# Four-layer transformer on one core: semaphores declared in another order, two bits to a bisection step in the last mixture's routing, and gathered rows added inside the fourth batch

## Chip, core and metric

One core of a Trainium2 chip runs the whole program in one launch. The metric is the device time of that launch in microseconds; the time of a kernel is the median of its runs. Engines are called as in the profile: PE is TensorE (PEld its weight loads), DVE is VectorE, ACT is ScalarE, POOL is GpSimd, SP is SyncE, which only issues transfers here.

## What is computed

Four layers in sequence on 4096 tokens of 128 features (4 batches of 1024). Each layer is `x = x + attention(xn) + ffn(xn)` with `xn = layernorm(x)`. The change touches the mixtures of experts of layers 0 and 2, above all the one of layer 2, the last mixture of the program:

```python
def _L2_attn_ref(x, ...):                # gated attention, squared relu scores
    kernel = jnp.square(jax.nn.relu(qk / sqrt_s))
    out = u * jnp.einsum('bij,bje->bie', kernel, v)
    return x * res_scale + out @ o_w.T

def _L2_ffn_ref(x, router_w, wg, wu, wd):
    capacity = max(1, int(CF * N / E))   # 640 rows for each of 8 experts
    probs = jax.nn.softmax(logits, axis=-1)
    topw, topi = jax.lax.top_k(probs, K) # two experts a token
    topw = topw / (topw.sum(-1, keepdims=True) + 1e-06)
    order = jnp.lexsort((-fw, fe))       # by expert, the heaviest first
    keep = rank < capacity               # lighter ones fall out
    ...                                  # experts on the kept rows
    out = jnp.zeros_like(xf).at[st].add(contrib)
```

## The kernel before, in words

The program is a row of stages. In each, every engine has its own instruction stream; an `order()` generator of the stage is walked by each engine's function, so that all of them meet the same steps (`"score"`, `"apply"`, ...) in the same sequence. Engines wait for each other through named signals (`sig(name)`), each one hardware semaphore, declared at first use; a `then()` makes DVE wait for its own last result first. `pe_products` is the signal that PE raises, `act_done` ACT's, `dve_done` DVE's, and `rows_sent`, `row_in*` and `expert_in*` are raised by transfers.

Layer 2 is `layer_two()`: a normalisation stage, then `unit([0, 1, 2])` (attention of the first three batches, with the routing of all tokens and the sending of rows to the experts inside), then `mix.experts()`, then `unit([3])` (attention of the fourth batch, with the experts' rows gathered meanwhile and added).

- **A batch in `unit`**: steps `v`, `u`, then for each of 8 blocks `jb` a `score` (PE lines L1909, ACT L1969 and L1973) for the next block and an `apply` (PE L1919) for this one, then `gate` (DVE L2014) and `out` (PE L1930, DVE L2023). `base` (PE L1894) and the two `turned` (DVE L1991 to L2001) prepare the next batch. PE's products L1900 open a batch with `v`.
- **Routing**: `route_dve` and `route_pe` are generators; a `"count"` step in `order()` moves PE's one step, a `"route"` step DVE's. The 640th largest weight of each expert is found by bisection on the bits of its float, 30 bits, one to a step: DVE sets a bit in the threshold (L938), compares all 4096 x 8 weights (L939), adds the hits of a partition (L940); PE sums over partitions by a product with ones (L837); DVE tests against 640 and keeps the bit or not (L944 to L946). Then come ranks among ties, a count above, ranks of the kept, and two passes that make the row numbers (`picks`, ending at L984). `order()` gives three count and route steps to a block: before `score`, before `apply` and after it.
- **Sending**: once `picks` is there, POOL issues 64 indirect transfers (L991, `send`) that scatter the 4096 rows, twice, to `GX` in DRAM. `experts` waits for all of them.
- **The fourth batch**: POOL gathers rows of `GY` (L1000, `gather`), two transfers for each of 32 chunks `ch`, into a ring `RB` of NR = 8 chunks; from the ninth chunk on it waits until DVE has added chunk `ch` - 8. DVE adds a chunk (`combine`, L1019, two instructions) and takes its statistics (`row_stats`, L769). In the kernel before, all 32 chunks (step `"row"`) stand behind the `out` of the batch.

Layer 0 has the same mixture with a simpler routing; its 64 sends run beside its shared expert (PE L1166, L1169, L1178; ACT L1191; DVE L1204).

Of the kernel before, what the change touches and what calls it, by code (L numbers as in the profile page):

```python
# [6 lines left out]
F32 = mybir.dt.float32  # L7
# [137 lines left out]
def program(nc, a, out):  # L145
    ctx = ExitStack()
    with ctx:
# [623 lines left out]
        class Mixture:  # L771
# [3 lines left out]
            def __init__(self, c, c1, pre, names, router, second, slots):  # L775
                self.pre, self.names, self.router, self.second, self.slots = pre, names, router, second, slots
                self.WE = [sig(f"expert_in{i}") for i in range(slots)]
# [31 lines left out]
            def route_tiles(self, c):  # L809
                (self.LG, self.E1, self.O1, self.O2, self.MK, self.TP, self.W, self.K1, self.K2, self.CN) = [  # L810
                    sb([128, NC, 8], c=c) for _ in range(10)]
                self.PF = [sb([128, NC, 8], c=c) for _ in range(2)]
                self.m, self.p1, self.p2 = [sb([128, NC], c=c) for _ in range(3)]
                self.TH, self.TC, self.MI = [sb([128, 8], I32, c) for _ in range(3)]
                self.cnt = sb([128, 8], c=c)
# [4 lines left out]
            def route_pe(self, e):  # L820
# [14 lines left out]
                def count(key):  # L835
                    e.wait_ge(DV, key)
                    e.op.matmul(PS[:, 3, 0:8], self.ones[:], self.cnt[:], start=True, stop=True).then_inc(*PM.up(key))  # L837
# [3 lines left out]
                else:  # L841
                    for bit in range(29, -1, -1):
                        count(("count", bit))
                        yield
                    ranks("ties", self.O2)
                    yield
                    count("above")
# [10 lines left out]
            def route_dve(self, e):  # L858
                LG, E1, O1, O2, MK, TP, W, K1, K2, CN = (self.LG, self.E1, self.O1, self.O2, self.MK, self.TP, self.W,
                                                         self.K1, self.K2, self.CN)  # L860
                PF, m, p1, p2, TH, TC, MI, cnt = (self.PF, self.m, self.p1, self.p2, self.TH, self.TC, self.MI,
                                                  self.cnt)
# [29 lines left out]
                def best(p, O):  # L892
# [6 lines left out]
                best(p1, O1)  # L899
# [3 lines left out]
                best(p2, O2)  # L903
# [29 lines left out]
                else:  # L933
                    then().memset(TH[:], 0).then_inc(*DV.up())
                    thb = TH[:].bitcast(F32).unsqueeze(1).broadcast_to([128, NC, 8])
                    tcb = TC[:].bitcast(F32).unsqueeze(1).broadcast_to([128, NC, 8])
# [16 lines left out]
                    then().tensor_reduce(cnt[:], O1[:].rearrange("p c e -> p e c"), AX, ALU.add).then_inc(  # L953
# [3 lines left out]
                    e.op.tensor_copy(cnt[:], PS[:, 3, 0:8]).then_inc(*DV.up())  # L957
                    cb = cnt[:].unsqueeze(1).broadcast_to([128, NC, 8])
# [64 lines left out]
            def experts(self, also_pool=None, also_sp=None):  # L1023

                ws, WE, slots, YE = self.ws, self.WE, self.slots, self.YE
                with ExitStack() as c:
# [4 lines left out]
                    GL = [sig(f"group_in{i}") for i in range(3)]  # L1031
# [680 lines left out]
        def layer_two():  # L1712
# [3 lines left out]
            with ExitStack() as c:  # L1716
# [82 lines left out]
                def unit(bs):  # L1799
# [3 lines left out]
                    with ExitStack() as c1:  # L1803
# [13 lines left out]
                        def order():  # L1817
# [10 lines left out]
                            for b in bs:  # L1828
                                for jb in range(8):
# [7 lines left out]
                                    yield "count", b, jb  # L1837
                                    yield "route", b, jb
# [947 lines left out]
```

## Time and profile before

| | us |
|---|---|
| median of 3 runs | 5004.88 (4992.2 to 5011.04) |
| the profiled execution's own time | 5011.82 |
| its span, first to last instruction | 5010.0 |
| PE busy | 3596.1 (72%) |
| DVE busy | 3088.8 (62%) |
| ACT busy | 2703.4 (54%) |
| POOL busy | 1078.8 (22%) |

The table's busy shares are averages over all stages. The stretch that the change touches runs from about 3711 us (start of the first `unit`) to 4292 us (end of the second) on the span's clock. Matmuls of f32 stand twice in the trace (two passes each), so that a `score` is 4 records, an `apply` 8, an `out` 32.

### The profile page before, as it was taken

What the parts mean: (1) busy time and instruction counts of PE and PEld (TensorE: products, weight loads), DVE (VectorE), ACT (ScalarE), POOL (GpSimd) and SP (SyncE); (2) the same over time, 40 slices, a digit from 0 to 9 for tenths busy, and PEclk for the clock granted to TensorE, in tenths of its full rate; (3) what the DMA queues carried; (4) which work ended last, traced back from release to release, by engine and by line L of the source; (5) the groups of instructions that cost most, each with busy time, mean ns of one, the idle gap of its engine ahead of it and who ended that gap; (6) DMA issues with size and microseconds to landing.
All of it is one profiled execution on the core that took longest, in us unless ns stands there. A gap on an engine that the chain in (4) does not pass through costs nothing. (4 is left out here: it accounts for less than half of the span.)

```text
span 5010.0 us, 51751 instructions
## 1 busy us (share of the span) xinstructions
PE 3596.1 (72%) x19476; PEld 1721.7 (34%) x19476; DVE 3088.8 (62%) x4918; ACT 2703.4 (54%) x3832; POOL 1078.8 (22%) x1105
## 2 busy tenths in 40 slices
PE   6795788878757877777779997899767596631125
PEld 4372111111111111111127775677643264211114
DVE  4123888888435656565568885788755232368876
ACT  2120576667559889899966763677432222212224
POOL 1302471010021010100003230222110503108770
PEclk8796899999767777776779999999978798765557
DMA  4011121000010010100000000000020011440001
GB/s 126 23 35 37 33 51 27 17 24 14 4 41 23 13 24 5 23 13 13 1 15 1 1 1 18 3 1 1 6 72 0 34 53 30 63 54 0 9 0 30
DMA packets 110179, 117.81 MB, mean 24 GB/s; under 512 B 20476, under 2 KB 81896, under 8 KB 109928
## 3 DMA queue, kind: packets, MB, share of 16 engines
q1 hardware_dynamic: 101736, 97.71, 8.8%
q0 software_dynamic: 8192, 16.79, 1.4%
q8 instruction: 153, 2.51, 0.2%
q14 instruction: 98, 0.80, 0.1%
HBM read 65.62 MB, written 33.82 MB: 20 GB/s over the span
## 5 line engine op out<-in xcount | busy, mean ns | idle before, releaser
L417 PE MATMUL PS<-t 48*128 48x512 bf16 (+1 forms) x3072 | 882.4, 462 | 427.2 <-ACT t L543 128.6
L525 ACT ACTIVATE t<-PS 128x512 f32<-128x512 f32 x1024 | 553.7, 595 | 249.6 <-PE PS L417 245.7
L567 DVE TENSOR_REDUCE t<-PS 128x1 f32<-128x1024 f32 x512 | 621.4, 1221 | 108.0 <-PE PS L409 98.4
L628 DVE TENSOR_TENSOR t<-t 128x1536 f32<-128x1536 f32 (+1 forms) x384 | 585.7, 1589 | 152.7 <-ACT t L543 94.3
L417 PEld LDWEIGHTS PS<-t 48*128 48x128 bf16 (+1 forms) x3072 | 164.3, 97 | 1361.2 <-ACT t L525 460.4
L484 PE MATMUL PS<-t 128*9 128x512 f32 x4096 | 593.8, 655 | 3.7 <-DVE t L628 3.5
L543 ACT ACTIVATE t<-PS,t 128x1536 f32<-128x1536 f32 (+1 forms) x384 | 504.7, 1418 | 44.3 <-PE PS L417 41.1
L545 ACT ACTIVATE t<-PS 128x1536 f32<-128x1536 f32 (+1 forms) x384 | 474.0, 1311 | 58.2 <-PE PS L417 55.6
L1582 POOL TENSOR_TENSOR t<-t 128x512 f32<-128x512 f32 x128 | 225.1, 1778 | 1214.3 <-DVE t L1512 1214.3
L409 PE MATMUL PS<-t 48*128 48x512 bf16 x1024 | 358.6, 403 | 44.0 <-DMA t<-scr 23.2
L2326 PE MATMUL PS<-t 128*128 128x32 f32 x256 | 61.1, 403 | 391.8 <-ACT t L2361 296.9
L1458 ACT ACTIVATE t<-PS,t 128x192 f32<-128x192 f32 x512 | 166.6, 437 | 182.0 <-DVE t L1541 182.0
L640 DVE RECIPROCAL t<-PS 128x16 f32<-128x16 f32 x64 | 16.5, 258 | 323.4 <-PE PS L492 322.8
L1359 PE MATMUL PS<-t 128*128 128x512 f32 x384 | 188.4, 629 | 26.4 <-ACT t L1458 12.5
L2382 ACT COPY t<-PS 128x640 f32<-128x640 f32 x64 | 44.3, 692 | 294.9 <-DVE PS L2436 290.3
L2326 PEld LDWEIGHTS PS<-t 128*128 128x128 f32 x256 | 56.9, 328 | 397.3 <-ACT t L2361 301.6
L1401 PE MATMUL PS<-t 128*128 128x65 f32 x1024 | 191.9, 278 | 0.9 <-DVE t L1551 0.9
L991 POOL DMA_INDIRECT scr<-t x128 | 126.0, 984 | 302.6 <-DVE t L984 264.3
L1000 POOL DMA_INDIRECT t<-scr,t x128 | 123.7, 966 | 253.3 <-DMA scr<-t 182.0
L1403 PE MATMUL PS<-t 128*128 128x65 f32 x896 | 173.2, 275 | 0.0
L214 PE MATMUL PS<-t 128*128 128x128 f32 x288 | 48.5, 344 | 164.5 <-ACT t L206 132.4
L2462 POOL TENSOR_TENSOR t<-t 128x256 f32<-128x256 f32 x128 | 102.5, 801 | 271.5 <-ACT t L2382 264.0
(371 smaller groups left out, 6844.2 us busy)
## 6 DMA issues: line engine op xcount, KB each, us to landing
t<-scr SPq DMA_DIRECT2D x384, 64.0 KB
scr<-t SPq DMA_DIRECT2D x96, 128.0 KB
t<-t SPq DMA_DIRECT2D x16, 512.0 KB, 10.6
scr<-t SPq DMA_DIRECT2D x2, 2560.0 KB
t<-scr SPq DMA_DIRECT2D x16, 320.0 KB, 3.7
scr<-t SPq DMA_DIRECT2D x16, 320.0 KB, 2.7
t<-in_L_ffn_rg_dram SPq DMA_DIRECT2D x8, 256.0 KB, 6.2
t<-in_L_ffn_ru_dram SPq DMA_DIRECT2D x8, 256.0 KB, 5.9
```

The source lines that it names most:

```text
L409: t = e.op.matmul(PS[:, 2 * side + hf, :], Qx[p // 4 % 2][lo:lo + KP, j, qc * 128:qc * 128 + 128], Kx[p // 4 % 2][lo:lo + KP, j, hf * 512: ...
L417: return e.op.matmul(PS[:, bk, :], Kx[p // 4 % 2][lo:lo + KS, j, kb * 128:kb * 128 + 128], Qx[p // 4 % 2][lo:lo + KS, j, hf * 512:hf * 512 ...
L484: t = e.op.matmul(PS[gq:gq + 9, PVB, :], Vx[p // 8 % 2][:, kb, 8 * side + p % 8, :], src, start=kb == 0, stop=kb == 7)
L525: e.op.activation(P[x % 4][:, 2 * hf + side, :], PS[:, 4 + hf, :], ACT.Exp, scale=S8).then_inc(*PW.up((p, k, side, hf)))
L543: t = e.op.activation(dst, PS[:, bk:bk + nu, :], ACT.Sigmoid, bias=extra[0], scale=S8)
L545: t = e.op.activation(dst, PS[:, bk:bk + nu, :], ACT.Exp, scale=S8)
L567: e.op.tensor_reduce(MX[p % 2][:, side, qc:qc + 1], PS[:, 2 * side:2 * side + 2, :].rearrange("p a n -> p (a n)"), AX, ALU.max).then_inc(* ...
L628: e.op.tensor_tensor(o, o, SGM[(12 * p + 3 * blk + ti) % 3][:, 0:nu, :], ALU.mult).then_inc(*DG.up((p, blk, ti)))
L1359: e.op.matmul(PS[:, j, :], xs, wqkv[:, 512 * j:512 * j + 512], start=True, stop=True).then_inc(*PM.up(("proj", n, j)))
L1401: t = e.op.matmul(o, PTC[i][:, h, :], V[:, n % NV, h, :], start=True, stop=fresh)
L1403: t = e.op.matmul(o, PTP[i][:, h, :], V[:, (n - 1) % NV, h, :], start=False, stop=True)
L1582: e.op.tensor_tensor(sn[:, :, :, lo:lo + 32], x[:, :, :, 32 - lo:64 - lo], TS[:, pc, :, lo:lo + 32].unsqueeze(2).broadcast_to([128, 2, 8, ...
```

## The change

Three things. **Semaphores**: `group_in*` and `expert_in*` are declared earlier and `rows_sent` last, so that these signals, and `row_in*`, lie on other semaphore numbers. **Bisection**: the threshold advances by two bits a step. DVE makes three candidates (bit patterns 1, 2, 3 at that place), compares against all three into a tile of three planes, and reduces them in one instruction to 24 counts; PE sums 24 columns; DVE multiplies each candidate by its test and takes the largest. 15 steps in place of 30. **Order**: the third count and route step of a block is gone, in the first `unit` too; in the fourth batch the blocks 2 to 7 now hold two `"row"` steps each, so that chunks 0 to 11 are added there and chunks 12 to 31 behind `out`.

```diff
-        RT, GZ, SENT, SH = sig("route_in"), sig("zeros_out"), sig("rows_sent"), sig("shared_in")
+        RT, GZ, SH = sig("route_in"), sig("zeros_out"), sig("shared_in")
         GYS = [sig(f"group_out{i}") for i in range(2)]
+        GL = [sig(f"group_in{i}") for i in range(3)]
+        WE8 = [sig(f"expert_in{i}") for i in range(8)]
         NR = 8
         GR = [sig(f"row_in{i}") for i in range(NR)]
+        SENT = sig("rows_sent")
...
-                    for bit in range(29, -1, -1):
-                        count(("count", bit))
+                    for bit in range(28, -1, -2):
+                        count(("count", bit), 3)
                         yield
...
-                    for bit in range(29, -1, -1):
-                        then().tensor_scalar(TC[:], TH[:], 1 << bit, None, ALU.bitwise_or).then_inc(*DV.up())
-                        then().tensor_tensor(TP[:], W[:], tcb, ALU.is_ge).then_inc(*DV.up())
-                        then().tensor_reduce(cnt[:], TP[:].rearrange("p c e -> p e c"), AX, ALU.add).then_inc(
+                    for bit in range(28, -1, -2):
+                        e.wait_ge(DV)
+                        for k in range(3):
+                            e.op.tensor_scalar(TC[:, k, :], TH[:], (k + 1) << bit, None, ALU.bitwise_or).then_inc(
+                                *DV.up())
+                        e.wait_ge(DV)
+                        for k in range(3):
+                            e.op.tensor_tensor(
+                                GE[:, k, :, :], W[:],
+                                TC[:, k, :].bitcast(F32).unsqueeze(1).broadcast_to([128, NC, 8]), ALU.is_ge).then_inc(
+                                *DV.up())
+                        then().tensor_reduce(cnt[:], GE[:].rearrange("p k c e -> p k e c"), AX, ALU.add).then_inc(
                             *DV.up(("count", bit)))
                         yield
                         e.wait_ge(PM, ("count", bit))
-                        e.op.tensor_scalar(MI[:], PS[:, 3, 0:8], float(CAP), None, ALU.is_ge).then_inc(*DV.up())
-                        then().tensor_scalar(MI[:], MI[:], bit, None, ALU.logical_shift_left).then_inc(*DV.up())
-                        then().tensor_tensor(TH[:], TH[:], MI[:], ALU.bitwise_or).then_inc(*DV.up())
+                        e.op.scalar_tensor_tensor(
+                            out=cnt[:], in0=PS[:, 3, 0:24].rearrange("p (k e) -> p k e", k=3), scalar=float(CAP),
+                            in1=TC[:].bitcast(F32), op0=ALU.is_ge, op1=ALU.mult).then_inc(*DV.up())
+                        then().tensor_reduce(best[:], cnt[:].rearrange("p k e -> p e k"), AX, ALU.max).then_inc(
+                            *DV.up())
+                        then().tensor_tensor(TH[:].bitcast(F32), TH[:].bitcast(F32), best[:], ALU.max).then_inc(
+                            *DV.up())
...
                                     yield "apply", b, jb
-                                    yield "count", b, jb
-                                    yield "route", b, jb
+                                    if not route and jb > 1:
+                                        yield "row", b, 2 * jb - 4
+                                        yield "row", b, 2 * jb - 3
...
                             if not route:
-                                for ch in range(NC):
+                                for ch in range(12, NC):
                                     yield "row", last, ch
```

The first place is a bisection step on DVE, in the first `unit`. In the kernel before (threshold bit, compare, add up, then test, shift, set):

```order
L938 TENSOR_SCALAR t<-t 128x8
L939 TENSOR_TENSOR t<-t 128x256
L940 TENSOR_REDUCE t<-t 128x8
L944 TENSOR_SCALAR t<-PS 128x8
L945 TENSOR_SCALAR t<-t 128x8
L946 TENSOR_TENSOR t<-t 128x8
```

The same place in the changed kernel (line numbers are its own; PS is the sum that PE left):

```order
L947 TENSOR_SCALAR t<-t 128x8 x3
L951 TENSOR_TENSOR t<-t 128x256 x3
L955 TENSOR_REDUCE t<-t 128x24
L959 SCALAR_TENSOR_TENSOR t<-PS,t 128x24
L962 TENSOR_REDUCE t<-t 128x8
L964 TENSOR_TENSOR t<-t 128x8
```

Six instructions for a bit have become ten for two bits.

The second place is PE in the blocks of the first batch. Before, L837 is the sum over partitions, L1909 `score`, L1919 `apply`:

```order
L837 MATMUL PS<-t 128x8 x2
L1909 MATMUL PS<-t 128x512 x2
L837 MATMUL PS<-t 128x8
L1919 MATMUL PS<-t 128x512 x4
L837 MATMUL PS<-t 128x8 x2
L1909 MATMUL PS<-t 128x512 x2
```

In the changed kernel L844 is that sum, L1928 `score`, L1938 `apply`:

```order
L844 MATMUL PS<-t 128x24
L1928 MATMUL PS<-t 128x512 x2
L844 MATMUL PS<-t 128x24
L1938 MATMUL PS<-t 128x512 x4
L844 MATMUL PS<-t 128x24
L1928 MATMUL PS<-t 128x512 x2
```

The two sums that stood back to back behind `apply` have become one.

The third place is DVE in the fourth batch. Before: the two edges of the scores, the gate, the two adds of `out`, and then the chunks of rows:

```order
L2007 TENSOR_TENSOR t<-PS,t 128x512 x2
L2014 TENSOR_TENSOR t<-PS,t 128x1024 x2
L2023 TENSOR_TENSOR t<-PS,t 128x512 x2
L1019 SCALAR_TENSOR_TENSOR t<-t 128x128 x2
L769 BN_STATS t<-t 128x6
L1019 SCALAR_TENSOR_TENSOR t<-t 128x128 x2
```

In the changed kernel (here the start of the twelve chunks; the last lines are those behind the twelfth):

```order
L2026 TENSOR_TENSOR t<-PS,t 128x512 x2
L1038 SCALAR_TENSOR_TENSOR t<-t 128x128 x2
L772 BN_STATS t<-t 128x6
...
L1038 SCALAR_TENSOR_TENSOR t<-t 128x128 x2
L772 BN_STATS t<-t 128x6
L2033 TENSOR_TENSOR t<-PS,t 128x1024 x2
L2042 TENSOR_TENSOR t<-PS,t 128x512 x2
L1038 SCALAR_TENSOR_TENSOR t<-t 128x128 x2
```

Twelve chunks have moved ahead of the gate; POOL's own instructions stand in the same order in both kernels.

## Rows read from the trace of the kernel before

**Rows 1.** Busy time by stretch: stretch, length, PE, PEld, DVE, ACT, POOL, PE clock, DMA share, GB/s

```profile
3754.00:3872.00 118.00, 91.85 (x247) 45.48 (x246) 67.59 (x199) 34.45 (x50) 0.00 (x0) 0.86 0.00 0
3902.00:3926.00 24.00, 24.00 (x80) 13.17 (x80) 13.14 (x13) 11.17 (x20) 19.02 (x17) 1.00 0.13 44
3926.00:3989.00 63.00, 9.45 (x26) 4.28 (x24) 0.82 (x2) 1.41 (x2) 45.09 (x47) 0.61 0.15 50
4224.00:4292.00 68.00, 0.00 (x0) 0.00 (x0) 31.49 (x95) 0.00 (x0) 45.60 (x48) 0.52 0.24 47
```

**Rows 2.** Timeline of DVE, a bisection step: start us, length us, instruction, idle before it

```profile
3765.12 0.42 DVE L939 TENSOR_TENSOR t<-t 128x256 f32<-128x256 f32 x1
3765.58 0.61 DVE L940 TENSOR_REDUCE t<-t 128x8 f32<-128x256 f32 x1
3766.67 0.17 DVE L944 TENSOR_SCALAR t<-PS 128x8 int32<-128x8 f32 x1 [0.48 <-PE PS L837]
```

**Rows 3.** Groups by line, another reduction of DVE, of as many elements

```profile
L893 DVE TENSOR_REDUCE t<-t 128x32 f32<-128x256 f32 x2 | 0.8, 420 | 0.1
```

**Rows 4.** Timeline of PE, one block of the first batch

```profile
3764.13 1.96 PE L1909 MATMUL PS<-t 128*128 128x512 f32 x4
...
3772.27 0.39 PE L837 MATMUL PS<-t 128*128 128x8 f32 x2 [1.98 <-DVE t L940]
```

**Rows 5.** Timeline of DVE, from a `turned` to the bisection's next instruction

```profile
3801.30 0.81 DVE L1991 TENSOR_SCALAR t<-t 128x1024 f32<-128x1024 f32 x1
...
3806.66 0.16 DVE L944 TENSOR_SCALAR t<-PS 128x8 int32<-128x8 f32 x1
```

**Rows 6.** Timeline of PE, marks in the second batch and the third's start

```profile
3842.72 3.70 PE L1900 MATMUL PS<-t 128*128 128x256 f32 x16
...
3854.98 0.29 PE L837 MATMUL PS<-t 128*128 128x8 f32 x2
...
3887.23 0.59 PE L832 MATMUL PS<-t 128*128 128x256 f32 x2
...
3901.40 1.88 PE L1909 MATMUL PS<-t 128*128 128x512 f32 x4
...
3906.55 1.88 PE L1909 MATMUL PS<-t 128*128 128x512 f32 x4
...
3915.13 3.62 PE L1900 MATMUL PS<-t 128*128 128x256 f32 x16
```

**Rows 7.** Timeline of POOL, the first and the last of 64 sends

```profile
3901.68 1.58 POOL L991 DMA_INDIRECT scr<-t  x1 [166.98 <-DVE t L984]
...
3984.34 0.96 POOL L991 DMA_INDIRECT scr<-t  x1 [0.30 <-issue]
```

**Rows 8.** Timelines of DVE (two rows) and ACT (one) during the sends

```profile
3944.82 0.69 DVE L2023 TENSOR_TENSOR t<-PS,t 128x512 f32<-128x512 f32 x1 [19.13 <-issue]
3988.87 0.69 DVE L2023 TENSOR_TENSOR t<-PS,t 128x512 f32<-128x512 f32 x1 [43.35 <-remote]
3991.68 0.69 ACT L1969 ACTIVATE t<-PS,t 128x512 f32<-128x512 f32 x1 [64.24 <-PE PS L1909]
```

**Rows 9.** Waits, layer 0: total us, times, longest

```profile
DVE t L1204 <- remote: 44.2, 5, 10.5
```

**Rows 10.** Timelines of the fourth batch: POOL, ACT, DVE, POOL, DVE

```profile
4167.28 0.99 POOL L1000 DMA_INDIRECT t<-scr,t  x1 [181.98 <-DMA scr<-t]
...
4186.10 0.94 POOL L1000 DMA_INDIRECT t<-scr,t  x1 [0.30 <-issue]
...
4189.91 1.27 ACT L1969 ACTIVATE t<-PS,t 128x512 f32<-128x512 f32 x2 [6.50 <-remote]
...
4214.94 2.36 DVE L2014 TENSOR_TENSOR t<-PS,t 128x1024 f32<-128x1024 f32 x2 [38.84 <-PE PS L1919]
...
4224.46 0.94 POOL L1000 DMA_INDIRECT t<-scr,t  x1 [37.42 <-DVE t L1019]
...
4291.18 0.29 DVE L769 BATCH_NORM_STATS2 t<-t 128x6 f32<-128x128 f32 x1 [0.35 <-DVE t L1019]
```

More of the change, by code:

```diff
@@ L776, in __init__ @@
                 self.pre, self.names, self.router, self.second, self.slots = pre, names, router, second, slots
-                self.WE = [sig(f"expert_in{i}") for i in range(slots)]
+                self.WE = WE8[:slots]
                 self.held = [f"expert_in{i}" for i in range(slots)]
@@ L809, in route_tiles @@
             def route_tiles(self, c):
-                (self.LG, self.E1, self.O1, self.O2, self.MK, self.TP, self.W, self.K1, self.K2, self.CN) = [
-                    sb([128, NC, 8], c=c) for _ in range(10)]
+                tiles = sb([128, 10, NC, 8], c=c)
+                (self.LG, self.E1, self.TP, self.O1, self.O2, self.MK, self.W, self.K1, self.K2, self.CN) = [
+                    tiles[:, i] for i in range(10)]
+                self.GE = tiles[:, 0:3]
                 self.PF = [sb([128, NC, 8], c=c) for _ in range(2)]
                 self.m, self.p1, self.p2 = [sb([128, NC], c=c) for _ in range(3)]
-                self.TH, self.TC, self.MI = [sb([128, 8], I32, c) for _ in range(3)]
-                self.cnt = sb([128, 8], c=c)
+                self.cnt = sb([128, 3, 8], c=c)
+                if self.second:
+                    self.TH, self.TC = sb([128, 8], I32, c), sb([128, 3, 8], I32, c)
+                    self.best = sb([128, 8], c=c)
             def flat(self, x):
@@ L833, in ranks, with count @@
                         *PM.up((tag, "sums")))
-                def count(key):
+                def count(key, n):
                     e.wait_ge(DV, key)
-                    e.op.matmul(PS[:, 3, 0:8], self.ones[:], self.cnt[:], start=True, stop=True).then_inc(*PM.up(key))
+                    e.op.matmul(PS[:, 3, 0:8 * n], self.ones[:], self.cnt[:, 0:n, :].rearrange("p c e -> p (c e)"),
+                                start=True, stop=True).then_inc(*PM.up(key))
                 if not self.second:
@@ L846, in route_pe @@
                     yield
-                    count("above")
+                    count("above", 1)
                     yield
@@ L890, in route_dve, with first_of @@
                 then().tensor_tensor(E1[:], E1[:], bc(m), ALU.mult).then_inc(*DV.up())
-                def best(p, O):
+                def first_of(p, O):
                     then().tensor_reduce(p[:], LG[:], AX, ALU.max).then_inc(*DV.up())
@@ L898, in route_dve @@
                 then().tensor_copy(LG[:], E1[:]).then_inc(*DV.up())
-                best(p1, O1)
+                first_of(p1, O1)
                 yield
@@ L902, in route_dve @@
                                             op1=ALU.add).then_inc(*DV.up())
-                best(p2, O2)
+                first_of(p2, O2)
                 yield
@@ L952, in route_dve @@
                     ranks("ties")
-                    then().tensor_reduce(cnt[:], O1[:].rearrange("p c e -> p e c"), AX, ALU.add).then_inc(
+                    then().tensor_reduce(cnt[:, 0, :], O1[:].rearrange("p c e -> p e c"), AX, ALU.add).then_inc(
                         *DV.up("above"))
@@ L956, in route_dve @@
                     e.wait_ge(PM, "above")
-                    e.op.tensor_copy(cnt[:], PS[:, 3, 0:8]).then_inc(*DV.up())
-                    cb = cnt[:].unsqueeze(1).broadcast_to([128, NC, 8])
+                    e.op.tensor_copy(cnt[:, 0, :], PS[:, 3, 0:8]).then_inc(*DV.up())
+                    cb = cnt[:, 0, :].unsqueeze(1).broadcast_to([128, NC, 8])
                     then().tensor_tensor(CN[:], CN[:], cb, ALU.add).then_inc(*DV.up())
@@ L1030, in experts @@
                     SG = [sb([128, 2, 320], c=c) for _ in range(3)]
-                    GL = [sig(f"group_in{i}") for i in range(3)]
                     def order():
```

7 lines of the change are left out of this document (3 added, 4 removed).

## The prediction, on record before the run

> **What bounds the kernel now.** I read three views. First the busy time by stretch, to see which engine carries each part of layer 2. While the bisection runs, PE is busy 91.85 of 118 us and DVE 67.59: neither is full, they wait for each other. Right behind it, 3902 to 3926 us, PE is full (24.00 of 24.00). Then comes the oddest stretch of the layer: from 3926 to 3989 us PE is busy 9.45 of 63 us, DVE 0.82 and ACT 1.41; only POOL works. The last stretch, 4224 to 4292 us, has no PE at all, only DVE and POOL [rows 1].
>
> Second, the timelines of DVE, PE and POOL, to see who waits in each. In the bisection one step is a closed loop over DVE and PE, and PE, which takes its stream in order, stands behind it. In the odd stretch DVE waits 19.13 and 43.35 us to add two products of `out`, and ACT 64.24 us for a `score` [rows 8]. PE had run all three by 3928 us; what came late is the raise of its signal. It stays late until 3988.84, that is 3.6 us behind the end of the last send [rows 7]. In layer 0, beside its 64 sends, DVE waits 10.5 us before nearly each product, to five times 44.2 us, released by something that the profile doesn't name [rows 9]. So: while POOL issues indirect transfers back to back, PE's signals reach the others late. In the second `unit` this shows in small: 16 gathers run from 4167.28 on, and ACT stands 6.50 us until 4189.91, 2.9 us after the last of the sixteen ended [rows 10]. I call this the lag.
>
> Third, the waits of POOL in the fourth batch: it stops after 16 gathers for 37.42 us, until DVE comes to the first chunk behind `out`; then 48 gathers at 1.25 us each set the pace to the end of the stage at 4291.5 [rows 1, 10].
>
> **The change part by part.**
>
> *Semaphore order.* It adds and removes no instruction. I cost it at nothing; no work needs to hide it. It could only act through the lag, which is a rival below.
>
> *A bisection step.* Before: from compare at 3765.12 to its test at 3766.67, with a test, a shift, a set and a bit of 0.17 and 0.03 between them each, 2.36 us for a bit. After, for two bits: three ORs of 0.2 are 0.6; three compares of 0.43 are 1.3; the reduction has three times the elements. The strided one of before takes 0.61 us for 256 elements [rows 2], a plain one 0.42 [rows 3], so 768 elements cost between 3 x 0.42 = 1.26 and 3 x 0.61 = 1.84. I take 1.5: it is the strided kind, and pays its start once. PE's answer costs the 0.48 of before, and the three closing operations 0.65 (one of them a small reduction that has no row; it is between 0.17 and 0.42). Sum 4.5 us, bounds 4.3 and 4.9. By the Trainium skill (VectorE: DVE Perf Modes, The TRN2 errata) an f32 `tensor_tensor` of DVE takes (N + 151) / 0.96 ns for N elements, an estimate of 0.96 us for 768 elements, and the sum would be 8 us lower over the steps; for 256 elements it gives 0.42, which the plain reduction meets and the strided one does not, so the row decides.
>
> *PE's side of it.* Before, a block with three bits takes from 3764.13 to 3772.5, 8.4 us, against 5.15 us for a block without any [rows 4, 6]. After, a block has two steps with a `score` behind one and an `apply` behind the other. A `score` takes 1.9 us by its row, 1.7 where the next product overlaps it, which leaves 3.4 of the 5.15 for the `apply`; both are shorter than 4.5, so DVE's loop is the clock: 9.0 us a block for four bits.
>
> *First batch.* First sum at 3757.5 (2 us later than now, the first mask is longer). The fifteenth is 14 steps on, 3820.5; `base` behind the fourth block adds 2.4 (3.4 + 3.4 on PE against 4.5), and the two `turned` 5.4 each on DVE [rows 5]: 3833.7. Test and tie mask 2.5, ranks on PE 1.2, the eighth `apply` 3.4: the second batch's `v` starts at 3840.8, where it is 3842.72 now [rows 6]. Only 2 us, because DVE does the same work in half the steps.
>
> *Second batch.* `v`, `u`, a score and `out` take 12.3 us (3842.72 to 3854.98) in both. Now the batch then still holds six sums, the ties, the count above and the kept ranks. After, only the count above and the kept ranks are left, both in the first block: kept ranks on PE end at 3858.3 (now 3887.8). From there `apply` 3.4, six blocks of 5.15, `base` 3.4 and a last `apply` 3.4: `v` of the third batch starts at 3899.4, against 3915.13. Gain 15.7 us; with the reduction at its bounds 13 to 19 (14 steps of 0.2 or 0.4 us).
>
> *The sends.* First send 13.9 us behind the kept ranks [rows 6, 7]: 3872.2, 29.5 us earlier. 64 of them take 83.6 us, to 3955.8. The lag began 24 us and 80 matmul records into the sends [rows 1]; the same gives 3896 to 3959, again 63 us long, again well inside the `unit`, so PE loses the same 54 us (63 less 9.45). It moves, and I count 0 for it, bounds -8 and +8 (where in a batch it falls; `v` and `u` are now inside it). So the first `unit` gains 16.
>
> *The fourth batch.* DVE adds chunk 0 once it has landed, and it has nothing else to do between the edges and the gate: 38.84 us, up to 4214.94 [rows 10]. POOL therefore no longer stops after 16 gathers: chunks 8 to 11 follow as DVE frees the ring, and then eight more, chunks 12 to 19, to 40 gathers, at 1.25 us each until 4217.5. Chunks 0 to 11 are added by about 4200, 15 us ahead of the gate, so no wait of DVE for a landing is on the path. Behind `out` there are then 24 gathers in place of 48: 24 x 1.25 = 30 us less.
>
> But the lag now has 34 us more of gathers to live in, from 4186 to 4217.5 plus 2.9. In layer 0 two products (4 records) pass in 11.2 us, 2.8 us a record [rows 9]; a block of the fourth batch has 12 records, so 33.6 us for what takes 5.15. In 34 us PE gets one block and the head of the next done, some 6 us of work. 28 us are lost, `out` ends near 4251 instead of 4223, and the 30 us come off from there. Net -2, bounds -30 (no lag) and +5 (lag from the first gather). By the Trainium skill (TensorE: Matmul & The Clock Gate, The cost: per-tile semaphore tail) sixteen increments at the end of matmuls cost a tail of about 0.5 us; by that estimate there would be no lag and the time would be that of the first rival. The trace does not agree, with 43.35 us.
>
> Sum: -16 and -2 are -18. Made against the profiled execution: 5011.8 - 18 = 4993.8. That execution stands 6.9 above the median of the three runs, so as a median 4987.
>
> **Rivals.**
>
> *The gathers do not lag, or hardly.* For it: the sixteen gathers of now cost ACT one wait of 6.50 us, of which some 2.5 is the ordinary one, and PE nearly nothing; the sends write to DRAM, the gathers to SBUF. Against: that wait ends 2.9 us after the last gather, just as those in the sends do. Then -16 - 30 = -46: 4959.
>
> *The lag starts with the first transfer.* In layer 0 it began within 10 us. Place: the sends at 3872 and the gathers at 4167. Price: up to 21 us more in the first `unit`, 14 more in the fourth batch: -18 + 35 = +17, 5022, slower than before. It decides from 18 us of extra lag in sum on. Against: the lag seems to need a store of waiting records, 80 in 24 us before.
>
> *The order of the semaphores is what the lag hangs on.* Then it ends in both layers: -16, -54, some -60 in layer 0 and -30: near 4845. For it: in the first lag PE's signal and `rows_sent` are close together in number. Against: in the gathers the signals are others (`row_in*`) and the lag is there too, and plain transfers that raise semaphores far oftener bring none.
>
> **How the numbers follow.** Forecast 0.60, its own range 4970 to 5003 (-35 to -2: the bounds of the sends' lag and of the reduction added); no lag in the gathers 0.25; lag from the first transfer 0.10; semaphores 0.05. The time is the forecast's, 4987. The range takes in the first rival with its bound and stops short of the two others: 4948 to 5008. A measurement of this kernel tells about 0.5% (25 us) from no change. Faster by more than that: 0.25 + 0.05 + a third of the forecast's 0.60 = 0.48 with a little off for the first rival's edge. Slower by more: a part of the second rival, 0.06. The rest, 0.46, is within.
>
> **What would show it.** In the changed profile: sums of the bisection 4.5 us apart; 15 of them; first send near 3872; third `v` near 3899; a stretch of some 60 us with an idle PE, ending 3.6 us behind the last send. In the fourth batch: 40 gathers without a stop; ACT waiting for scores for 30 us and more behind the 16th gather; `out` near 4251; then 24 gathers; the stage's length as before within 5 us. The prediction is wrong if ACT goes on at its pace beside the gathers (then the time is near 4959), if bisection sums are over 5.5 us apart (the first `unit` gains nothing), or if the lag has another length than the sends.

## The result, and the profile of the changed kernel

| | before | changed |
|---|---|---|
| median of 8 runs each, us | 5004.6 (4992.2 to 5015.7) | 4978.4 (4966.7 to 4991.5) |
| ratio, 95% interval | | 0.9941 (0.9926 to 0.9956) |
| the profiled execution | 5011.8 | 4991.5 |
| mean granted clock of PE in it | 0.82 | 0.82 |

26 us less, where 18 were predicted (4987, range 4948 to 5008). The profiled execution of the changed kernel is one of its longest: its first `unit` starts 10.0 us later than before (first product of the logits at 3721.45 against 3711.45 us), in stages that the change doesn't touch. So 10.0 us are taken off below wherever a time of the changed kernel is set against one of before.

**The bisection.** Timelines of the changed kernel, first of DVE (one step and the start of the next), then of PE.

```profile
3777.52 0.18 DVE L959 SCALAR_TENSOR_TENSOR t<-PS,t 128x24 f32<-128x24 f32 x1 [1.70 <-PE PS L844]
3777.74 0.18 DVE L962 TENSOR_REDUCE t<-t 128x8 f32<-128x24 f32 x1
3777.95 0.17 DVE L964 TENSOR_TENSOR t<-t 128x8 f32<-128x8 f32 x1
3778.16 0.32 DVE L947 TENSOR_SCALAR t<-t 128x8 int32<-128x8 int32 x3
3778.51 1.10 DVE L951 TENSOR_TENSOR t<-t 128x256 f32<-128x256 f32 x3
3779.64 1.53 DVE L955 TENSOR_REDUCE t<-t 128x24 f32<-128x768 f32 x1
3781.67 0.18 DVE L959 SCALAR_TENSOR_TENSOR t<-PS,t 128x24 f32<-128x24 f32 x1 [0.49 <-PE PS L844]
```

```profile
3771.97 5.38 PE L1938 MATMUL PS<-t 128*128 128x512 f32 x8
3777.19 0.30 PE L844 MATMUL PS<-t 128*128 128x24 f32 x2
3777.33 1.96 PE L1928 MATMUL PS<-t 128*128 128x512 f32 x4
3781.23 0.40 PE L844 MATMUL PS<-t 128*128 128x24 f32 x2 [1.94 <-DVE t L955]
3781.47 5.38 PE L1938 MATMUL PS<-t 128*128 128x512 f32 x8
3786.69 0.30 PE L844 MATMUL PS<-t 128*128 128x24 f32 x2
```

DVE's step is 4.15 us from test to test when PE answers at once (3777.52 to 3781.67, a wait of 0.49). But in most blocks only every second step is that short. In the other the sum has to queue behind an `apply` of 5.38 us, and DVE's test waits 1.70 us for it, as in the first row. A block of four bits takes 9.50 us (3777.19 to 3786.69). In one block the `apply` takes 3.68 us (from 3790.97 on), and there both steps are 4.15.

**The sends.** Busy time by stretch, changed kernel (columns as in [rows 1]), then timelines of DVE (first three rows) and ACT.

```profile
3883.40:3916.00 32.60, 32.60 (x85) 15.86 (x84) 12.96 (x12) 15.17 (x24) 25.59 (x24) 1.00 0.13 45
3916.00:3926.00 10.00, 6.21 (x24) 2.75 (x22) 0.00 (x0) 2.39 (x4) 7.60 (x8) 1.00 0.15 52
3926.00:3971.00 45.00, 3.89 (x18) 2.33 (x18) 0.69 (x1) 2.37 (x3) 31.59 (x33) 0.57 0.14 50
```

```profile
3928.60 0.69 DVE L2026 TENSOR_TENSOR t<-PS,t 128x512 f32<-128x512 f32 x1 [15.49 <-remote]
3971.36 0.69 DVE L2042 TENSOR_TENSOR t<-PS,t 128x512 f32<-128x512 f32 x1 [42.06 <-remote]
...
4028.12 0.82 DVE L1140 COPY t<-PS 128x640 f32<-128x640 f32 x1 [4.34 <-PE PS L1092]
3974.95 0.69 ACT L1988 ACTIVATE t<-PS,t 128x512 f32<-128x512 f32 x1 [43.91 <-PE PS L1928]
```

The lag is there again ([rows 8] show it before): PE full for 32.6 us, then an `out` whose signal DVE gets 42 us late, 4 us behind the last send's end (3967.4). But it is shorter. In the 87 us from the first send until the signals are back PE was busy 33.5 us before (24.00 and 9.45 in [rows 1]) and is busy 42.7 now (32.60, 6.21 and 3.89). The experts' first flip (L1140) comes 118.0 us behind `v` of the third batch (3910.1), where it took 133.5. (Here and below `v` is the start of its first weight load, up to 0.4 us ahead of its first product, which is what [rows 6] show.)

**The fourth batch.** Timelines of POOL (two rows), ACT (two) and DVE (three), changed kernel, beside [rows 10].

```profile
4148.06 0.99 POOL L1019 DMA_INDIRECT t<-scr,t  x1 [180.67 <-DMA scr<-t]
...
4236.65 0.94 POOL L1019 DMA_INDIRECT t<-scr,t  x1 [38.77 <-DVE t L1038]
4184.58 0.69 ACT L1988 ACTIVATE t<-PS,t 128x512 f32<-128x512 f32 x1 [20.41 <-issue]
...
4204.22 1.26 ACT L1988 ACTIVATE t<-PS,t 128x512 f32<-128x512 f32 x2 [12.27 <-remote]
4226.93 2.36 DVE L2033 TENSOR_TENSOR t<-PS,t 128x1024 f32<-128x1024 f32 x2 [45.91 <-PE PS L1938]
...
4234.85 0.69 DVE L2042 TENSOR_TENSOR t<-PS,t 128x512 f32<-128x512 f32 x1 [1.09 <-PE PS L1949]
4272.10 2.22 DVE L188 BATCH_NORM_AGGREGATE t<-t 128x2 f32<-128x6 f32 x32 [2.24 <-PEq L122]
```

POOL issues 40 gathers until 4197.9 and stops once. ACT waits 20 and 12 us for scores. `out` ends 90.0 us behind `v` (4145.5), 31.4 later than before (58.6), and the next stage starts 36.6 us behind it instead of 68.8: 32.2 given back of 31.4 lost.

### The profile page after: what moved, and what is told of

Its sections match the earlier page's. It is cut to its first block and busy times, and to the rows that moved or that the text cites. A ratio compares the mean times of both kernels' runs of the same rounds, so it can differ in the third digit from the quotient of the medians.

```text
span 4989.6 us, 51661 instructions
## 1 busy us (share of the span) xinstructions
PE 3599.8 (72%) x19446; PEld 1715.8 (34%) x19446; DVE 3088.3 (62%) x4888; ACT 2702.5 (54%) x3832; POOL 1077.9 (22%) x1105
## 5 line engine op out<-in xcount | busy, mean ns | idle before, releaser
L1600 POOL TENSOR_TENSOR t<-t 128x512 f32<-128x512 f32 x128 | 225.1, 1777 | 1214.5 <-DVE t L1530 1214.5
L2401 ACT COPY t<-PS 128x640 f32<-128x640 f32 x64 | 44.3, 692 | 295.2 <-DVE PS L2455 290.6
L2345 PEld LDWEIGHTS PS<-t 128*128 128x128 f32 x256 | 56.9, 328 | 398.2 <-ACT t L2380 301.9
L1419 PEld LDWEIGHTS PS<-t 128*128 128x128 f32 x1024 | 150.6, 191 | 15.2 <-issue 13.9
```

The costliest lines, as they stand in the source:

```text
L1419: t = e.op.matmul(o, PTC[i][:, h, :], V[:, n % NV, h, :], start=True, stop=fresh)
L1600: e.op.tensor_tensor(sn[:, :, :, lo:lo + 32], x[:, :, :, 32 - lo:64 - lo], TS[:, pc, :, lo:lo + 32].unsqueeze(2).broadcast_to([128, 2, 8, ...
```

## The experiments

Twelve kernels in four groups (e1 to e4, e5 to e8, e9 and e10, e11 and e12); every ratio is to the kernel before, run beside the group on the same chip. The three times are read from the timelines as above: layer 0's first flip on the span's clock; `v` of the third batch to the first flip of layer 2; `v` of the fourth batch to the next stage (`BATCH_NORM_AGGREGATE`).

| kernel | ratio (95%) | layer 0's flip | third `v` to flip | fourth `v` to next stage |
|---|---|---|---|---|
| before | | 288.3 | 133.5 | 127.4 |
| changed | 0.9941 (0.9926 to 0.9956) | 289.7 | 118.0 | 126.6 |
| e1_semaphores | 0.9996 (0.9982 to 1.0009) | 290.7 | 128.5 | 126.4 |
| e2_bisection | 0.9935 (0.9917 to 0.9952) | 292.6 | 115.5 | 126.2 |
| e3_rows | 0.9991 (0.9977 to 1.0004) | 292.7 | 127.9 | 124.1 |
| e4_gathers_paced | 0.9876 (0.9853 to 0.9899) | 287.8 | 117.6 | 101.8 |
| e5_sends_paced | 0.9835 (0.9820 to 0.9850) | 290.4 | 86.6 | 107.9 |
| e6_all_paced | 0.9740 (0.9724 to 0.9757) | 240.2 | 81.1 | 102.6 |
| e7_sends_late | 0.9970 (0.9958 to 0.9982) | 287.7 | 128.1 | 126.8 |
| e8_sends_blind_pauses | 0.9852 (0.9831 to 0.9873) | 290.6 | 93.3 | 105.1 |
| e9_sends_behind_out | 0.9944 (0.9931 to 0.9958) | 223.4 | 111.1 | 94.7 |
| e10_stops_at_down | 0.9865 (0.9850 to 0.9880) | 224.8 | 70.6 | 94.7 |
| e11_changed_again | 0.9871 (0.9847 to 0.9895) | 224.9 | 70.6 | 94.6 |
| e12_stops_again | 0.9868 (0.9845 to 0.9892) | 225.1 | 70.7 | 94.7 |

The last four rows are of another kind; e9 below tells why.

### e1, e2, e3: one part alone

```diff
 # e1_semaphores: the kernel before with these lines
+        GL = [sig(f"group_in{i}") for i in range(3)]
+        WE8 = [sig(f"expert_in{i}") for i in range(8)]
...
+        SENT = sig("rows_sent")
 # e2_bisection: the changed kernel without them, and with
-                                    if not route and jb > 1:
-                                        yield "row", b, 2 * jb - 4
-                                        yield "row", b, 2 * jb - 3
...
-                                for ch in range(12, NC):
+                                for ch in range(NC):
 # e3_rows: the kernel before with
+                                    if not route and jb > 1:
+                                        yield "row", b, 2 * jb - 4
+                                        yield "row", b, 2 * jb - 3
...
-                                for ch in range(NC):
+                                for ch in range(12, NC):
```

> The kernel before with only the semaphores declared in the new order. My theory: the numbers of the semaphores carry nothing. Ratio to the kernel before 1.000 within 0.001; in the trace the waits of 40 us and more beside the sends of layer 0 and of the first unit are all there. Rival (the third rival of the prediction, or a smaller form of it): the order shortens the late signals; then at least the 10 us by which the sends cost less after the change show here, 0.998 or lower, and 0.97 if they vanish.

> The change without the new order of the semaphores and without rows added inside the fourth batch: two bits to a step and two steps to a block alone. My theory: this is where the time comes from, all of it: the first unit is 27 to 30 us shorter (15 from the route that ends earlier, 14 from sends that hold PE up for less), ratio 0.9943 to 0.9950, and the fourth batch is as before. Rival: the route alone is worth its 16 us (0.9968), and the rest of the 26 us came from one of the two other parts.

> The kernel before with rows 0 to 11 added inside the fourth batch, nothing else. My theory: POOL then issues 40 gathers without a stop, PE's signals come some 30 us late, the end of out is 30 us later and 24 gathers instead of 48 stand behind it: -1 us, ratio 0.9995 to 1.0005. Rival: no late signals when this part stands alone; then -30 us, 0.994.

e1: 0.9996, and the lag stands. In its timeline of ACT the score behind the sends is as late as in [rows 8]:

```profile
3985.16 0.69 ACT L1971 ACTIVATE t<-PS,t 128x512 f32<-128x512 f32 x1 [58.83 <-issue]
```

e2 holds the whole gain (0.9935, its interval takes in 0.9941). e3 holds none that can be told from nothing (0.9991, interval up to 1.0004), and its ACT waits the same way inside the fourth batch:

```profile
4206.28 0.69 ACT L1972 ACTIVATE t<-PS,t 128x512 f32<-128x512 f32 x1 [16.86 <-remote]
...
4229.39 1.27 ACT L1972 ACTIVATE t<-PS,t 128x512 f32<-128x512 f32 x2 [15.73 <-remote]
```

So the three parts add up within their intervals, and the 40 gathers without a stop are where the rows' gain is lost, as e4 shows next. The table also says that the sends cost the profiled execution of before more than they cost e1 and e3: 133.5 us from third `v` to flip there, 128.5 and 127.9 here. From the first batch's `v` to the flip the three kernels with the old route took 321.5, 316.6 and 312.6, the three with the new one 289.8, 285.4 and (e4) 289.6: 28.6 us between the means. And in the 87.3 us from the first send on PE was busy 33.8, 38.1 and 36.8 us in the first three and 42.7, 45.2 and 45.5 in the others.

### e4: gathers in step with ACT

```diff
+                                    if ch in range(2, 18, 2):
+                                        e.wait_ge(AC, ("square", last, ch // 2 - 1))
                                     mix.gather(e, RB, ch)
```

> The changed kernel, but in the fourth batch POOL issues the gathers of two chunks (four transfers, 5 us) for each block, and waits before each pair for ACT's square of the block before. My theory: the signals of PE are late only while POOL issues without a pause, and late signals themselves now stop POOL, so that the backlog can run off: out ends 60 to 72 us behind v instead of 90, some 36 to 40 gathers are done by then or shortly after, and the kernel is 15 to 25 us faster than the changed one (ratio to before 0.989 to 0.991). Rival: pauses as short as these don't help, the signals stay late with POOL standing: out ends at 90 us as now, with fewer gathers done, and the kernel is 5 to 15 us slower than the changed one (0.996 to 0.998).

More than expected: 0.9876, and 24.8 us less from `v` to the next stage than in the changed kernel. POOL stood for ACT only twice; these are the two rows of its timeline, from the second gather to the end of `out`, with an idle time over 1 us:

```profile
4143.43 0.98 POOL L1019 DMA_INDIRECT t<-scr,t  x1 [4.35 <-ACT t L1994]
...
4167.31 0.94 POOL L1019 DMA_INDIRECT t<-scr,t  x1 [4.17 <-ACT t L1994]
```

The first is the start. The second is the lag beginning: ACT had waited 6.16 us for a score until 4161.75, POOL stopped 4.2 us for it, and from there to the gate ACT waits 5.41 us at most, behind an `apply` of 6.70. With these stops `out` ends 65.3 us behind `v` and not 90.0.

### e5, e6: the sends in step too

```diff
 def send(self, e, pace={}):
...
+                    if ch in pace:
+                        e.wait_ge(AC, pace[ch])
 # e5: e4, and in layer 2 before every second chunk or so
+ pace = {2: ("square", 1, 4), 6: ("square", 1, 5), 8: ("square", 1, 6), 10: ("square", 1, 7), 12: ("v", 2, 7), 16: ("square", 2, 0)}
+ pace.update({2 * jb + 18: ("square", 2, jb) for jb in range(1, 7)})
 # e6: e5, and in layer 0 as well: chunks 2, 4 and so on wait for ACT's product (j, f) of about that time
+ pace = {2: (2, 7), 4: (3, 0)}
+ for m in range(4):
+     pace.update({8*m+6: (3+m, 3), 8*m+8: (3+m, 6), 8*m+10: (3+m, 7), 8*m+12: (4+m, 0)})
```

> The kernel with paced gathers, and now also the 64 sends of layer 2 in steps of four: before each step POOL waits for the square (or v) of ACT that an undisturbed attention would just have reached. My theory: a wait of POOL of some 4 us lets the late signals out, as it did in the gathers, so that the sends hardly hold PE up; the sends end near 3970 on the clock of the changed kernel and the experts' first flip follows within 10 to 25 us in place of 61: 30 to 45 us less than with paced gathers alone, ratio to before 0.979 to 0.982. Rival: the scatters to DRAM behave otherwise than the gathers (it is the transfers in flight, not the issuing, that hold the signals), pauses don't help, and pace and late signals stop each other: sends end 20 us and more later, ratio 0.988 or higher.

> As the one before, and the 64 sends of layer 0 paced likewise by ACT's products of the shared expert. My theory: the same mechanism costs layer 0 about 60 us now (eight products of ACT take 65 us there instead of 14), and pacing gives back 35 to 50 of them: ratio to before 0.970 to 0.973. Rival: in layer 0 the signals are late within 10 us of the first send, sooner than in layer 2, so that waits after every fourth transfer stop POOL nearly each time and the sends stretch by as much as PE wins: within 10 us of the kernel before this one.

e5: 31.0 us less from third `v` to flip, but 6.1 more in the fourth batch than e4; net 20 us by the ratios of the two groups, less than the 30 to 45 expected (0.979 to 0.982), and outside the rival's 0.988 and more. e6: 50.2 us less in layer 0, at the edge of the 35 to 50 expected; 0.9740, where 0.973 was the upper bound and lies within the interval. These are all stops of POOL over 1 us between the first and the last send of layer 0:

```profile
107.52 0.96 POOL L1012 DMA_INDIRECT scr<-t  x1 [2.40 <-ACT t L1211]
135.56 0.96 POOL L1012 DMA_INDIRECT scr<-t  x1 [8.15 <-ACT t L1211]
162.31 0.95 POOL L1012 DMA_INDIRECT scr<-t  x1 [6.42 <-ACT t L1211]
187.46 0.96 POOL L1012 DMA_INDIRECT scr<-t  x1 [4.55 <-ACT t L1211]
```

One stop for each part of the shared expert, behind its `down`, 32 short products or 64 records of 128 columns. In three of these `down` (from 118.16, 147.60 and 174.62) PE runs 44, 49 and 53 records without a gap and then goes on for a while in ones to fours, 0.7 us and more apart; the one at 97.28, right behind the first send, runs all 64 in one go. So short products beside the sends look like what fills the backlog; no run separates them from the rest of the part.

### e7, e8: when, and what kind of stop

```diff
 # e7_sends_late: the changed kernel, and POOL behind `picks`
+                                e.wait_ge(AC, ("v", 2, 7))
 # e8_sends_blind_pauses: e4, and in layer 2's send
+                    if pause is not None and ch and ch % 4 == 0:
+                        for _ in range(3):
+                            e.wait_ge(PO)
+                            e.op.tensor_tensor(pause[:], pause[:], pause[:], ALU.subtract).then_inc(*PO.up())
```

> The changed kernel with its sends held back, about 30 us, until ACT has done v of the third batch; route and order of the batches as they are. Theory A, from the six traces so far: the first unit ends some 60 us behind the last send, whatever PE has done before, because little of the third batch passes while POOL issues; so the flip moves with the sends, 27 to 32 us later than in the changed kernel, and the ratio to before is 1.000 or a little over it. Theory B, which my prediction used: the sends take the same 54 us from PE wherever they lie, so that moving them costs 0 to 8 us: ratio 0.994 to 0.996.

> The kernel with paced gathers, and in the sends of layer 2 after every eighth transfer three idle operations of POOL of 1.3 us each on a tile of its own, about 4 us, without any wait for PE or ACT. My theory: what counts is that POOL stops issuing; the sends grow to 84 + 7 x 4.3 = 114 us and end near 3997, PE isn't held up, the flip comes at 4000 to 4010 in place of 4028: ratio to before 0.983 to 0.985. Rival 1: POOL must stand in a wait, being busy doesn't let the signals out; then sends end 30 us later and the flip with them: 0.993. Rival 2: pauses need to be longer than 4 us: as rival 1.

e7: neither theory. The sends start 32.0 us later against `v`, the flip comes 10.1 later than in the changed kernel, 14 us by the ratios. Busy time by stretch of e7:

```profile
3893.10:3900.00 6.90, 6.90 (x38) 4.75 (x37) 1.38 (x2) 4.52 (x7) 5.36 (x6) 1.00 0.14 47
3900.00:3977.00 77.00, 29.59 (x56) 11.50 (x54) 1.38 (x2) 7.24 (x9) 56.24 (x59) 0.70 0.15 51
```

Its sends begin in the middle of `u`, with `out` (16 short products, 32 records) right behind, and a first late signal (DVE, 4.85 us) is there 11 us behind the first send. Before, PE's full stretch ended 24 us behind it, in the changed kernel 32. By one measure for all, the end of the first product that ACT or DVE takes over 0.5 us late, it is 20 us before (24 in e1 and e3), 31 in the changed kernel (30 in e2 and e4) and 8 in e7. PE gets 36.5 us of work done beside these sends, 33.5 before, 42.7 in the changed kernel. So it is neither the end of the sends alone nor a fixed loss. What fits them is how much passes until the lag sets in; that is a reading of them, not a test of its own.

e8: 0.9852, a hair outside what was expected. POOL waits for nobody, yet PE's signals are hardly late: the most that DVE's adds of `out` wait longer than in a batch without sends is 1.1 us (2.27 and 2.18 at 3912.60 and 3915.47, where 1.15 and 1.04 are ordinary). The third batch's `out` is added at 3963.1, 62.7 us behind `v`. The sends take 109.9 us, and now they are the end, as its timeline of DVE shows:

```profile
3993.70 0.82 DVE L1144 COPY t<-PS 128x640 f32<-128x640 f32 x1 [30.59 <-PE PS L1096]
```

So a POOL that does something else for 4 us is as good as one that waits, and with runs of eight indirect transfers the lag hardly comes. Whether it is their issuing or the transfers in flight that must pause isn't separated, since both do.

### e9, e10: a group without the lag

```diff
 # e9_sends_behind_out: the changed kernel, and POOL behind `picks`
+                                e.wait_ge(AC, ("square", 2, 1))
 # e10_stops_at_down: e6, but in layer 0
+                    mix.send(e, {6 * m + 3: (3 + m, 0) for m in range(5)})
```

> The changed kernel with its sends held back by some 47 us, until ACT has done the second square of the third batch, so behind v, u and the 32 short products of out of the second batch. Theory: the lag is no matter of time since the first send (it came after 24, 32 and 10 us in three kernels) but of how many products PE issues while POOL issues: about 80 records. Behind the sends' start there are then only blocks of 12 records in 5.15 us, seven blocks or 36 us until the lag, so the third batch is nearly through before it; the unit ends with the sends, 105 us behind v of the third batch, and the flip at 108 to 115: sooner than in the changed kernel (118) and than with sends held back by 32 us (128), though it sends latest. Ratio to before 0.992 to 0.994. Rival: the lag begins at a time behind the first send and takes what is left of the batch, so that still later sends cost still more: flip at 130 to 145 behind v, ratio 0.997 to 1.000.

> The kernel with all three paced, but in layer 0 POOL sends six chunks (twelve transfers, 15.6 us) and then stands until ACT has the first product of the next of the eight parts of the shared expert, that is, over most of the 64 short products of down. In the kernel before this one the signals were late once a part, right behind down (ACT idle 12 to 17 us there where 8.3 is ordinary). Theory: short products fill the backlog, so a stop laid over them keeps the signals in time; 2 to 8 us less idle a part, the sends end near 201 and the first flip at 222 to 232 in place of 240: ratio 0.971 to 0.973. Rival: the stop that the late signals make by themselves is as good; the flip stays within 4 us of 240, ratio 0.974.

Both were meant for the question what fills the backlog, and neither can answer: the kernel before took 4895.1 us here, 2.2% less than beside the groups ahead, and in neither trace is there a single wait that ends with "remote", not even in e9's layer 0, where nothing was edited (flip at 223.4 instead of 288 to 293). In e9 the flip comes 10 us behind the last send, bound by the sends alone. The count of about 80 records stays a guess, and e7 speaks against it: from the first send to PE's first idle time of over 1 us there are 94 records in before, e1 and e3, 92, 88 and 88 in the changed kernel, e2 and e4, but 58 in e7.

### e11, e12: what the change is worth without the lag

No edit to the changed kernel in e11, none to e10's in e12.

> The changed kernel once more, since the last two kernels ran on another chip than the ones before, where the kernel before takes 4895 us instead of 5006 and no signal of PE was late in either trace. Theory: the late signals belong to some chips and not to others, and the change is worth another amount with and without them. On a chip with them: ratio 0.994 as before. On one without: the route that ends 15 us earlier and 24 gathers less behind out (30 us) both come off whole, with the third batch's end no longer tied to the sends: 45 us and more of 4895, ratio 0.989 to 0.991. Rival: the change is worth its 0.994 everywhere, and the last chip was faster for another reason.

> The kernel that stops POOL over down in layer 0 and paces the other two, once more beside the changed kernel on the same chip. On a chip with late signals, theory: first flip at 222 to 232 against 240 with the finer pacing and 288 unpaced, ratio to before 0.970 to 0.973. On a chip without: stops and pacing only cost, but nearly nothing, since sends and gathers end off the path: within 5 us of the changed kernel beside it, 0.9865 as last measured. Rival for the first case: 0.974 or more, the stops do no better than the waits that the late signals cause by themselves.

Again no lag (before at 4901.8), and the change is worth 0.9871, more than twice as much, 68 us between the medians. Its ratio's interval lies wholly below the one of the first result. Busy time beside the sends of layer 0, first the changed kernel with the lag, then the same kernel in e11:

```profile
98.00:182.00 84.00, 41.49 (x126) 20.42 (x126) 7.03 (x11) 4.78 (x8) 61.47 (x64) 0.63 0.15 50
```

```profile
98.00:182.00 84.00, 83.41 (x384) 53.02 (x385) 25.82 (x38) 18.97 (x32) 61.49 (x64) 1.00 0.15 51
```

Same kernel, same 64 transfers, same POOL time, same DMA share: PE does 41.49 us of work in one and 83.41 in the other. The granted clock is 0.63 where PE stands idle for half of the time and 1.00 where it is busy. In the fourth batch of e11 POOL issues its 40 gathers, stops 6.76 us and goes on right behind `out`:

```profile
4023.82 0.99 POOL L1019 DMA_INDIRECT t<-scr,t  x1 [128.81 <-DMA scr<-t]
...
4080.42 0.94 POOL L1019 DMA_INDIRECT t<-scr,t  x1 [6.76 <-DVE t L1038]
```

e12 stands at 0.9868: its stops and its pacing cost nothing that can be measured there (1.9 us between medians). Whether the stops at `down` beat the finer pacing where there is a lag was not measured.

## Why the prediction was right, and where it was not

- **Semaphore order, 0**: 0.9996. Right; the third rival is out.
- **A bisection step, 4.5 us; 9.0 a block**: the parts were 0.32 for the ORs (0.6), 1.10 for the compares (1.3), 1.53 for the reduction (1.5) and 0.49 for PE (0.48): 4.15 in all. The block was 9.50. What failed is "both are shorter than 4.5, so DVE's loop is the clock": in this stretch an `apply` takes 5.38 us, not 3.4. PE's granted clock is not full here, 0.82 and 0.82 in the two blocks from 3767.8 on and 0.87 over the whole of 3774 to 3883; I had taken the `apply` as what a block without a sum leaves, from a stretch at full clock. Small errors on either side met, which is luck: seven such blocks alone would put the fifteenth sum 3.5 us late, and it came at 3844.9, less 10 is 3834.9, against 3833.7.
- **Second batch 2 us earlier, third 15.7**: +0.8 and -14.6. The gain of the route was right.
- **First send at 3872.2**: 3883.4 less 10 is 3873.4.
- **The sends, "PE loses the same 54 us", 0 with -8 and +8**: the term that was mis-sized. The first `unit` gained 28.6 (means of three traces each), not 16. Up to the third `v` it gained 15.7 by the same means, as predicted; the other 12.9, beyond the bound of 8, lie between the third `v` and the flip, where the sends and the lag are. I had moved the lag by its time behind the first send (24 us). It doesn't go by time: it set in after 20, 31 and 8 us (before, changed, e7, by one measure). Sends that start earlier lie beside blocks of the second batch, with 6 long products (12 records) in 5.15 us, and PE gets 9 us more done beside them in the two profiled executions, 8 between the means of three.
- **The fourth batch, -2**: -0.8 (e3 alone: 3.3 less, within what traces differ by). Lag 31.4 predicted as 28, tail 32.2 shorter, predicted 30. Both terms came out, and e4 shows the cause by taking it away: -24.8. But the 28 was right by offset. PE got 11.7 us of work done from 4168 to 4201, not the 6 reckoned from 2.8 us a record; against that ACT's late scores spread over 40 us (4164.2 to 4204.2), not 34, and the next two `apply` took 5.32 and 6.54 us in place of 3.60.
- **The bounds**: 14 steps of 0.4 us more leave 10 of the 15.7 us, not 13. And -35 to -2 isn't the sum of the bounds that it names: with 13 to 19 they give -29 to -7. The measured -26 lies within either.
- **First rival (gathers do not lag, 4959)**: wrong in the runs that were predicted. In e11 its condition holds, by a reason that I hadn't as a case, that the lag can be absent altogether; its price, 46 us, does not, it is 68. Then the route gives 18 us (first to third `v`, 188.1 before, 169.9 in e11), the fourth batch 32.8 (127.4 to 94.6), and the flip is no longer tied to the end of the sends, estimated at 10: without the lag the old route's flip would come 10.1 us behind its last send (e9's distance), 80.7 behind `v`, against 70.6. Sum 61, measured 68 between medians. The old kernel has no trace without the lag, so this split is an estimate.
- **Second rival (lag from the first transfer)**: did not happen in layer 2.

What stays open: what holds PE's signals back, and when it is there. It isn't the kernel, and the records give the same chip number for a group with the lag (e1 to e4) and for one without (e11, e12). It holds for a whole group: the 48 executions of the kernel before beside the result, e1 to e4 and e5 to e8 took 4991 us and more, the 20 beside e9 to e12 at most 4915. No trace of the kernel before without the lag was taken.

The traces hold one clue that no run followed up, in their records of when a semaphore was raised. In e11 each raise by PE stands 0.02 us behind its product. In the changed kernel with the lag the second `out` of the second batch ends at 3930.26 on PE and its raise stands at 3971.28, so it is the raise that is late and not DVE. And raises are missing from the record there. In e9 to e12 the 64 sends of layer 2 leave 1024 raises, 16 for each; in the changed kernel 327 of them are recorded, before 257, in e7 169, in e8 with its pauses 796. ACT's and PE's own raises have gaps in the same stretch (18 of 31 and 22 of 34 recorded, all of them in e11) and none while the route runs. Late raises and missing ones go together, though e8 misses some with hardly a delay. Whether the number of raises, those of the transfers among them, is the cause, and whether the recording itself has a part in it, no run here shows.

## What to carry to other kernels

A long unbroken run of indirect transfers on POOL can hold up PE's signals until it ends (here for up to 43.35 us); look for rows that wait for "remote" or "issue" tens of us behind a product that PE has long issued. Break such a run with a wait for the engine that is fed by PE (as in e6: 0.9740 in place of 0.9941 with the lag; without it the nearest kernel, e12, whose layer 0 has longer stops, shows no measurable cost). That it should be kept away from stages of many short products is what e6 and e7 suggest, not a thing shown. And before pricing a change by a stall in one profile, find out whether the stall is always there: the same edit was worth 26 us with it and 68 without.

## What the runs showed of the hardware that was not expected

- The lag as such is not a property of a program: layer 0's first flip stood at 288 to 293 us in nine unpaced traces with it, at 240 with pacing, and at 223 to 225 in four without, which makes it worth about 65 us there. Over the kernel before it is 5006 against 4898 us.
- Stops of POOL of about 4 us keep it short: two in 40 gathers where POOL waits (4.35 and 4.17 us, e4), one after every eighth send where it is busy with something else (e8).
- With the lag the profile's record of semaphore raises has gaps beside indirect transfers (327 of 1024 for the sends of the changed kernel, 1024 of 1024 in e11). A wait that ends with "remote" goes with these gaps: e9 to e12, whose record is whole, have none.
- A small strided reduction of DVE (24 elements, L962) takes 0.18 us, as little as an elementwise instruction of 8; the strided one of 768 elements takes 1.53 us. For 768 elements the Trainium skill (VectorE: DVE Perf Modes, The TRN2 errata) gives (N + 151) / 0.96 ns for an f32 `tensor_tensor`, an estimate of 0.96 us; here the reduction over a strided view took 1.6 times that.
- The Trainium skill (TensorE: Matmul & The Clock Gate, The cost: per-tile semaphore tail) has a tail of about 0.5 us for sixteen increments. No run here tests that figure; the traces with the lag show a wait of 42.06 us for one `out`, some 80 times as long.
